# Local attention's mask: added by VectorE on the way to SBUF, where TensorE put it into the score bank before

## What is computed

```python
mask = (it < jb) | (it > jb + w) | (jb == -1)
sim = jnp.einsum('bhwie,bhwje->bhwij', bq, bk2) * QK_SCALE
sim = jnp.where(mask, -jnp.finfo(sim.dtype).max, sim)
attn = jax.nn.softmax(sim, -1)
out = jnp.einsum('bhwij,bhwje->bhwie', attn, bv2)
```

## Time and profile before

| | us |
|---|---|
| median of 3 runs | 5423.19 (5413.07 to 5423.49) |
| the profiled execution, whole | 5412.1 |
| its span | 5410.3 |
| PE busy | 5124.1 (95%) |
| VectorE busy | 3450.6 (64%) |
| ScalarE busy | 3047.6 (56%) |
| GpSimd busy | 2741.9 (51%) |

### The profile page before, as it was taken

How to read it: one execution, slowest core, us unless ns; L and a number is a source line. 1 busy time by engine, 2 the same in 40 slices (tenths; PEclk the granted TensorE clock), 3 DMA queues, 4 the chain that set the end, 5 groups by cost and what they waited for, 6 DMA issues and landing times. The chain is left out here.

```text
span 5410.3 us, 182888 instructions
## 1 busy us (share of the span) xinstructions
PE 5124.1 (95%) x68876; PEld 3086.6 (57%) x68876; DVE 3450.6 (64%) x6778; ACT 3047.6 (56%) x6413; POOL 2741.9 (51%) x2594
## 2 busy tenths in 40 slices
PE   8999999999999989999999999999999999999996
PEld 4556565555656555555555555555555555555553
DVE  3444444444444447777777777777777777777773
ACT  3445444443445446666666666666666666666663
POOL 1313232231313256666666666666666666666661
PEclk9999999999999989999999999999999999999997
DMA  1000000000000012111211221122111211121112
GB/s 28 6 3 4 3 4 3 4 3 3 5 3 4 3 35 54 47 47 54 55 47 47 59 55 46 46 55 55 47 47 44 64 47 47 47 67 45 46 44 61
DMA packets 140189, 186.79 MB, mean 35 GB/s; under 512 B 33719, under 2 KB 61514, under 8 KB 139482
## 3 DMA queue, kind: packets, MB, share of 16 engines
q1 hardware_dynamic: 139482, 176.16, 12.1%
HBM read 27.16 MB, written 4.19 MB: 6 GB/s over the span
## 5 line engine op out<-in xcount | busy, mean ns | idle before, releaser
L1080 POOL TENSOR_TENSOR cs<-cs 128x512 f32<-128x512 f32 x768 | 979.5, 1276 | 570.5 <-DVE cs L1391 566.8
L1207 PE MATMUL psum<-wqkv,xw 128*128 128x512 f32 x2304 | 1192.3, 609 | 30.9 <-POOL xw L1117 24.9
L1391 DVE TENSOR_TENSOR cs<-psum,rots 128x1024 f32<-128x1024 f32 x768 | 938.2, 1222 | 291.0 <-PE psum L1207 245.6
L1089 POOL TENSOR_TENSOR qk<-cs,rn 128x512 f32<-128x512 f32 x768 | 776.4, 1042 | 334.2 <-ACT rn L1273 289.5
L428 POOL TENSOR_SCALAR prob<-prob,rsum 128x128 f32<-128x128 f32 (+2 forms) x384 | 396.4, 1034 | 924.1 <-DVE rsum L761 923.9
L1289 ACT ACTIVATE sq<-psum 128x512 f32<-128x512 f32 x768 | 458.9, 598 | 650.1 <-DVE cs L1391 635.1
L755 DVE TENSOR_REDUCE negmax<-psum 128x1 f32<-128x128 f32 (+3 forms) x768 | 375.6, 489 | 641.6 <-PE psum L466 633.9
L608 ACT ACTIVATE prob<-psum,negmax 128x128 f32<-128x128 f32 (+3 forms) x768 | 404.3, 527 | 565.3 <-DVE negmax L755 554.6
L465 PE MATMUL psum<-kT,qz 128*128 128x128 f32 (+3 forms) x1536 | 604.4, 481 | 17.9 <-ACT qz L599 11.8
L1352 DVE TENSOR_REDUCE ss<-sq 128x8 f32<-128x512 f32 x768 | 519.9, 677 | 6.8
L1158 PEld LDWEIGHTS psum<-pT,vw 64*64 64x64 f32 x18624 | 401.4, 135 | 195.0 <-issue 194.3
(11 more groups left out here) (173 smaller groups left out, 8559.4 us busy)
## 6 DMA issues: line engine op xcount, KB each, us to landing
vw<-vl SPq DMA_DIRECT2D x768, 128.0 KB, 2.3
vw<-vl SPq DMA_DIRECT2D x672, 64.0 KB, 2.0
wqkv<-in_wqkv SPq DMA_DIRECT2D x42, 256.0 KB, 4.1
wol<-in_wol SPq DMA_DIRECT2D x7, 512.0 KB, 4.0
w1l<-in_w1l SPq DMA_DIRECT2D x7, 341.0 KB
x<-in_x SPq DMA_DIRECT2D x9, 256.0 KB, 2.8
sums<-sumout SPq DMA_DIRECT2D x8, 256.0 KB, 2.3
sums_in<-sums SPq DMA_DIRECT2D x8, 256.0 KB, 2.9
```

What stands on the lines that cost most here:

```text
L1080: summed_rot.done(nc.gpsimd.tensor_tensor(own, own, halves(cs[:, t % 2, j, 1, :])[:, :, ::-1, :], ALU.add), at)
L1089: rotated.done(nc.gpsimd.tensor_tensor(qk[:, j, :].rearrange("p (h c) -> p h c", c=EL), cs[:, t % 2, j, 0, :].rearrange("p (h c) -> p h c" ...
L1207: last = nc.tensor.matmul(ps[:, :], xw[:, t * P:(t + 1) * P], wqkv[:, col:col + BANK], start=True, stop=True)
L1391: parts.done(V.tensor_tensor(cs[:, t % 2, j, :, :].rearrange("p i (h c) -> p i h c", c=EL), twice, by_head, ALU.mult), at)
```

## The change

The two TensorE products of identity and mask at the head of each `sa` go, and the score products now start their banks themselves. VectorE's first step on a score bank is now an addition of the mask that writes to `probl` in SBUF; it signals `masked`, and that is what frees the bank. When both banks are in SBUF, the two maxima are taken from `probl`, and the two centers read `probl` and write it in place. Every center now reads two operands in SBUF (`probl` and the negated maxima) where it read a PSUM bank and one operand in SBUF.

```diff
@@ in transformer
+    masked = steps("masked", place("s"))
@@ readers of a bank
         if kind == "s":
-            return [(centered, at)]
+            return [(masked, at)]
@@ score_half
-                                start=False, stop=True, skip_group_check=True)
+                                start=True, stop=True, skip_group_check=True)
@@ PE, step sa
-                    mask = sh.maskw[:, min(t, 1), :].unsqueeze(1).to_broadcast([P, PAIRSL, WK])
-                    for p in range(PARITIES):
-                        nc.tensor.matmul(banks[p][:, :].rearrange("p (c k) -> p c k", k=WK), identb[:, :], mask,
-                                         start=True, stop=False, skip_group_check=True)
+                    settle(pe, passed)
                     score_half(t, banks, range(PAIRSL // 2))
@@ VectorE, center
                 centered.done(V.tensor_tensor(
-                    probl[:, t % 2, :, p, :], psum[ring.bank(("s", t, p))][:, :].rearrange("p (c k) -> p c k", k=WK),
+                    probl[:, t % 2, :, p, :], probl[:, t % 2, :, p, :],
                     negmaxl[:, t % 2, :, p].unsqueeze(2).to_broadcast([P, PAIRSL, WK]), ALU.add), (t, p))
@@ VectorE, step s
-                    maxed.done(V.tensor_reduce(negmaxl[:, t % 2, :, at[1]], ps[:, :].rearrange("p (c k) -> p c k", k=WK),
-                                               AX.X, ALU.max, negate=True), at)
+                    mask = sh.maskw[:, min(t, 1), :].unsqueeze(1).to_broadcast([P, PAIRSL, WK])
+                    masked.done(V.tensor_tensor(probl[:, t % 2, :, at[1], :], ps[:, :].rearrange("p (c k) -> p c k", k=WK), mask,
+                                                ALU.add), at)
                     if at[1] == 1:
+                        for p in range(PARITIES):
+                            masked.wait(dve, it, (t, p))
+                            maxed.done(V.tensor_reduce(negmaxl[:, t % 2, :, p], probl[:, t % 2, :, p, :], AX.X, ALU.max,
+                                                       negate=True), (t, p))
                         for p in range(PARITIES):
                             center(it, t, p)
```

More of the change, by code:

```diff
@@ L1336, in _ @@
         def _(dve):
-            for s in (parts, summed, clamped, maxed, centered, totalled, inverted, mid, ffn, hidden, left):
+            for s in (parts, summed, clamped, masked, maxed, centered, totalled, inverted, mid, ffn, hidden, left):
                 s.prime(dve)
```

## The result

The change makes the kernel slower. Its median is 5550.26 us (5547.38 to 5553.51, 4 runs), against 5422.27 (5413.07 to 5423.49, 4 runs) before: a ratio of 1.024, with a 95% interval of 1.0222 to 1.0258. That is +128 us where +38 was forecast, and it lies outside the range. The two profiled executions differ by 5545.6 - 5410.3 = 135 us in their spans.

A forecast was written before the change was run, and what follows sets the result against it. PE was taken as nearly full (486 of 500 us), with VectorE in a chain. Terms of -1.29, +1.25, +0.7 and +0.25 gave +0.91 us a trip, 44 us, taken as 40: 5460 us, range 5388 to 5500.

The forecast's parts named there:

- Masks, -1.29 a trip: PE's mask products: three of four pairs save 0.43 us each; `sa.3`'s buys nothing, as `t.0.2` waits for GpSimd.
- Durations: VectorE's softmax: two mask additions take 1.2 us a tile; maximum and center are no cheaper from SBUF.
- Waits of the centers: VectorE, tiles 3 and 0: second centers wait 0.86 us for GpSimd; tile 3's first 0.12, tile 0's first gets in.
- oa.2, +1.25: Tile 3: late centers delay ScalarE's copy of `v.0.1`, so PE loses 1.25 us a trip at `oa.2`.
- Tile 0, +0.7: Center and GpSimd waits cost PE 0.3 us at `t.1.2` and 0.4 at `pt.0.0`, 0.7 a trip together.
- rival C: Tile 0's delay runs on through VectorE's `qk.2.1` to `qk.2.3`, whose squares free banks: another 1 us a trip, 5508; chance 0.08.
- y2, +0.25: Tile 2: exponentials hold up the second gelu, so the trip's last product `y2` comes 0.25 us later.
- A: VectorE keeps the memory between its two centers, so a pair waits once: +0.25 us a trip, about 5433; chance 0.2.
- B: Centers in this form meet no contention with GpSimd: -30 us, 5393, or down to 5369; chance 0.2.
- D: The change does nothing, gain and loss within 11 us; no mechanism and no chance of its own.
- signs that I named: Expected in the records: PE's busy time about 147 us lower, some centers about 1.5 us, PE waiting at `oa.2` and `pt.0.0`.

The follow-up runs named there:

- e2: The changed kernel with TensorE's mask products kept as well, so the mask is added twice: 5689.05 us, ratio 1.0498.
- e4: The changed kernel with step `v.0.1` moved ahead of `s.3.0` and `s.3.1`, so ScalarE copies it before tile 3's exponentials: 5541.45 us, ratio 1.0217.
- e5: The changed kernel with one maximum per token and bank, given to the exponential as its bias, and no center: 5394.66 us, ratio 0.9965.
- g2: The changed kernel with GpSimd's three tensor operations of a trip cut to one of eight heads: 5393.88 us, ratio 0.9954.
- g1: The kernel before with GpSimd's three tensor operations of a trip cut to one of eight heads: 5380.02 us, ratio 0.9922.
- e1: The changed kernel with the mask added in place in the PSUM bank, which maximum and center read and a center frees: 5468.83 us, ratio 1.0095.
- e3: The kernel before with only the center's first operand changed from the bank to `probl` in SBUF, no instruction added: 5531.79 us, ratio 1.0197.
- the pads: 96 semaphore instructions ahead of PE's loop over layers: 5552.34 us on the changed kernel, 5425.32 us on the kernel before.

## Why the prediction was wrong in size

Direction and mechanism were right: centers with both operands in SBUF wait for GpSimd, and PE pays for it. Per trip the forecast was +0.91 us, and 2.79 were measured. The step that failed is the sum over PE's places. Its term for tile 0 was mis-sized, and three things had no term: the trips in which the centers of tile 3 meet GpSimd one instruction later, the lower clock behind them, and the gaps.

*Masks, -1.29 a trip.* Right: `sa.0`, `sa.1` and `sa.2` come 0.39 to 0.43 us earlier each. `sa.3` gives 0.46 and has lost all but 0.06 of it after `t.0.2`, as forecast. But e2, where that pair stands in front of the same softmax, has the long wait at `oa.2` in nearly every trip, so there it isn't free.

*Durations.* Right: addition 0.681, maximum 0.676, center 0.681 to 0.685 where GpSimd idles. The Trainium skill's fixed cycles (VectorE: DVE Perf Modes, the TRN2 errata) would have made SBUF sources 0.065 us shorter. The maximum takes 0.676 from SBUF and 0.681 from PSUM (medians of the source views), so the runs show 0.005 of that.

*Waits of the centers.* The second ones waited 0.85 us (1.527 - 0.681), forecast 0.86; tile 3's first 0.17, forecast 0.12. Tile 0's first waited 0.70, forecast next to nothing: it missed the gap between two products that I had it just catch.

*oa.2, +1.25.* Right for the usual trip: 1.30 (median), in the place and for the reason named. The mean, 1.39 + 0.14 at `t.0.3` = 1.53, is 0.28 higher because of the ten trips with the long wait: 14 us. The one trip that I worked out couldn't show them. e4 shows that the term was shared: had the copy been free, VectorE's own lateness would have taken 1.36 at `sa.0`.

*Tile 0, +0.7: mis-sized.* The 0.7 was 0.3 at `t.1.2` and 0.4 at `pt.0.0`. It measures 0.22 (`t.1.1`) + 0 (`t.1.2`) + 0.44 (`t.1.3`) + 0.69 (`pt.0.0`) = 1.35. At `t.1.2` nothing is lost, since the first center doesn't get ahead of GpSimd's third product but waits. Behind that wait `qk.2.0` is late too, and its square frees the bank of `t.1.3`. That is the start of rival C's chain, and it ends there: after `pt.0.0` no later square is waited for. In e5, without centers, both places lose under 0.1. This term is 0.65 x 48.25 = 31 us of the error of 1.88 x 48.25 = 91.

*y2, +0.25: right number, partly by luck.* It measures 0.28. But e5, whose exponentials don't wait for VectorE, loses nearly the same 0.27. ScalarE at this place in the kernel before:

```profile
3017.46 0.58 ACT L1291 COPY vl<-psum 128x512 f32<-128x512 f32 x1
3018.06 1.28 ACT L1319 ACT_TABLE_LOAD   x1
3019.35 0.69 ACT L1319 ACTIVATE gel<-psum,b1l 114x512 f32<-114x512 f32 x1
3020.05 1.28 ACT L1279 ACT_TABLE_LOAD   x1
3021.35 1.15 ACT L1279 ACTIVATE probl<-probl 128x512 f32<-128x512 f32 x2
3022.52 1.28 ACT L1319 ACT_TABLE_LOAD   x1
3023.81 1.26 ACT L1319 ACTIVATE gel<-psum,b1l 114x512 f32<-114x512 f32 x2
```

From the copy of `v.3.0` to the last gelu it has no pause over 0.02 us, and three table loads of 1.28 us are in that row. The copy stands behind a square that waits for VectorE, and before, after and in e5 it starts 3.68 us after PE's `qk.3.3` (medians). So the 0.43 us that PE gains at `sa.2` don't bring it forward. The second gelu starts 0.16 us later in the changed kernel (I had 0.75), because the exponentials wait 0.07 us for the center and overlap less, and 0.19 later in e5, where an exponential with a bias takes 0.72 instead of 0.63 us. About half of the 0.28 is this lateness, by my estimate, and the other half is ScalarE's own row, which PE now reaches earlier.

*The sum left out the gaps and the clock.* 54.4 - 20.5 = 34 us came from PE's runs of small products. Nearly 5 of them are in `s.3.0`, where they act through the wait at `oa.2` that is counted above, and about 30 are left. The lower clock behind the long waits is 16 us. No term or rival of mine had either. With tile 0's 31 and the 14 at `oa.2` this makes the 91. That it fits so closely is partly luck, since the parts overlap. Of the spans' difference of 135 us, 47 trips make 3379.5 - 3248.8 = 130.7. Another 6.5 lie ahead of the first trip, in the part that the change doesn't touch, and the tail is 1.9 shorter.

*Rivals.* A (VectorE keeps the memory) falls: both centers of a pair wait. B (no contention) falls by g2 against the changed kernel, and its time would not have been reached either: without contention g2 is still 14 us above g1. D falls. Of the signs that I named all but one came: PE's busy time fell by 16 us, not 147. That sign was ill made, for the two records of 0.38 us of a pair overlap and fill 0.43 us, so 83 us at most could go; e5's fell by 5124.1 - 5068.5 = 56. Of the other 40 of the changed kernel the clock explains an estimated 17: at half the clock a record takes twice as long, and in its trips the clock is low for 47.8 us, in e5's for 13.7, and half of the difference is 17. The remaining 23 stay open.

*The parts are no sum.* e1 has the additions alone and e3 the contention alone: +49 and +112 us, each with late banks (1.22 and 1.32 us a trip) that the change itself doesn't have. Together in the changed kernel they make 128, with the masks kept 269. Undoing one part moved the wait to another step each time, and only the comparison step by step showed it.

## What to carry to other kernels

A two-operand VectorE instruction whose operands both lie in SBUF took its own time here only while GpSimd was idle or nearly so (0.681 to 0.685 us, and up to 1.76 otherwise): before moving an operand from PSUM to SBUF, look at what GpSimd does at that moment, and count the wait for each of the two. Where the subtraction of a maximum can be given to ScalarE as a bias, the instruction goes altogether: with the center the mask's move lost 2.4%, and the kernel with the move and without the center (e5) is 0.35% faster than before. A sum over the places with slack needs each bank's reader and every instruction queued behind the late one; where three engines stand within a few tenths of a microsecond, a forecast wait at one place is only the first of several limits. And one trip isn't enough: where a wait depends on which instruction of another queue is met, a small delay can double it, so look at all trips before you take one as the rule.

## What the runs showed of the hardware

**The memory goes to the one that has waited, not to the one that is in the run.** Of two centers issued back to back the second loses to GpSimd's instruction that began to wait during the first: medians of 1.526 and 1.527 us against 0.681. GpSimd loses too, at each meeting about 0.45 us of its 1.04 (the four products of tile 3 take 4.50 instead of 4.04). The Trainium skill (SBUF — State Buffer, the section on SBUF's two separate sides) has the port pair go, for the whole instruction, to whoever starts first. The traces agree with that for each meeting, and add that a pair of instructions doesn't hold it together.

**The granted clock can fall behind a long wait of PE.** In the changed kernel it went from 1.00 to 0.50 for 3.4 to 6.8 us behind seven of ten waits of 2.1 to 2.5 us, and behind none of 36 of 1.01 us. In e2 it did so in 34 of 46 trips, all but one of which had waited 2.45 us. A projection took 2.07 us instead of 1.02.

**PE's runs of small products have gaps of their own, tied to places in the code.** They come back every eighth trip, and the pads move them. In the changed kernel all 75 gaps over 0.2 us end 1.19 to 1.60 us (median 1.39) after the end of one of the packets that bring instructions, and in the kernel before all 29 end 1.20 to 1.51 us after one. Its line in the DMA view of the changed kernel:

```profile
q8 instruction: 588, 9.63, 0.8%
```

588 packets of 16 KB, some ten a trip, most of them under way for 0.9 to 1.4 us. The Trainium skill (Runtime: NRT & Kernel Launch, instruction fetch mechanics) gives blocks of 16 KiB, 256 instructions each, and calls the cost of crossing one mostly hidden. The packet's size agrees. The cost doesn't here: 17 to 24 us of gaps in 46 trips with the mask products, 37 to 54 without them. That they come from instruction loading is argued from this timing and from the pads, and no run changed the loading itself; why eight long products a trip should halve them stays open.
